# A twelve-layer decoder on one core: the choice of tokens counts in the compare, the experts' norm moves to the middle stage, and gathers, adds, stores, expert products and unread products are put in another order

## The reference

```
scores = softmax(x @ gate_w.T)                    # 4096 tokens x 8 experts
kept_w, kept_idx = top_k(scores.T, k=512)         # each expert takes its 512 best tokens
y = x[kept_idx]
y = (y - mean(y)) * rsqrt(var(y) + 1e-5) * ln_w + ln_b
h = gelu(y @ fc1[e].T + b1[e])                    # 128 -> 512
out = (h @ fc2[e].T + b2[e]) * kept_w             # 512 -> 128
x = x.at[kept_idx].add(out)
```

## Time and profile before

| | us |
|---|---|
| median of 3 runs | 3353.27 |
| lowest, highest | 3339.86, 3361.25 |
| the profiled execution's own time | 3361.68 |
| its span, first to last instruction | 3359.5 |
| mean granted TensorE clock | 0.901 |
| PE busy | 2578.9 (77%) |
| PEld busy | 1833.1 (55%) |
| DVE busy | 1724.8 (51%) |
| ACT busy | 994.8 (30%) |
| POOL busy | 345.1 (10%) |

### The profile page before, as it was taken

The page is one execution under the profiler, slowest core; times in us unless marked ns, Lnnn a source line. Parts: engine busy times, 40 slices in busy tenths (PEclk is TensorE's granted clock), DMA queues, the critical chain, the costliest instruction groups (busy, mean ns, idle before and its releaser), DMA issues.

```text
span 3359.5 us, 52344 instructions
## 1 busy us (share of the span) xinstructions
PE 2578.9 (77%) x22728; PEld 1833.1 (55%) x22736; DVE 1724.8 (51%) x4110; ACT 994.8 (30%) x1385; POOL 345.1 (10%) x581
## 2 busy tenths in 40 slices
PE   4666468888888886366677779887798777987778
PEld 3444147777777775244555554655555555565554
DVE  5655735565665654631357541675416754167541
ACT  3333312222322221021132432324323243232432
POOL 0111100000000000065111000110001100011000
PEclk8788559999999998577898999989999899998999
DMA  2000000000000001112610000000000000000000
GB/s 81 1 1 1 2 1 1 8 8 8 1 8 8 8 8 48 45 30 44 160 40 1 1 7 0 1 1 1 7 0 1 1 1 7 0 1 1 1 1 25
DMA packets 39351, 48.09 MB, mean 14 GB/s; under 512 B 7169, under 2 KB 36369, under 8 KB 38354
## 3 DMA queue, kind: packets, MB, share of 16 engines
q1 hardware_dynamic: 33490, 40.43, 4.1%
q0 software_dynamic: 5632, 4.33, 1.0%
HBM read 31.81 MB, written 12.91 MB: 13 GB/s over the span
## 4 chain that ended last, share of the span: by engine, by line
PE 57%; DVE 30%; ACT 6%; issue 4%; POOL 2%; DMA 1%; SPq 0%; DVEq 0%; POOLq 0%; ACTq 0%
PE banks L2390 7%; PE banks L887 6%; DVE wide_area L2266 4%; PE banks L2589 3%; DVE wide_area L1744 2%; PE banks L2379 2%; PE banks L1387 2%; PE banks L2164 2%; PE banks L1352 2%; PE banks L1186 2%; DVE xs L916 2%; DVE weights L2083 1%; PE banks L1420 1%; PE banks L584 1%; PE banks L1671 1%
## 5 line engine op out<-in xcount | busy, mean ns | idle before, releaser
L2589 PE MATMUL banks<-wA 128*128 128x128 f32 x2362 | 317.7, 288 | 4.2 <-ACT xf L948 2.1
L2589 PEld LDWEIGHTS banks<-wA 128*128 128x128 f32 x2362 | 296.8, 202 | 23.4 <-issue 16.3
L908 DVE BATCH_NORM_STATS2 stats<-banks 128x6 f32<-128x128 f32 x208 | 46.3, 285 | 397.3 <-PE banks L887 362.9
L2266 DVE TENSOR_REDUCE wide_area<-banks 128x8 f32<-128x2048 f32 x64 | 146.7, 2293 | 106.7 <-PE banks L2164 106.7
L923 POOL TENSOR_TENSOR rstd<-moments,eps 128x4 f32<-128x4 f32 x56 | 11.1, 199 | 1438.4 <-DVE moments L912 1438.4
L2247 ACT ACTIVATE weights<-banks 128x2048 f32<-128x2048 f32 x64 | 120.1, 1877 | 99.2 <-PE banks L2173 99.2
L1744 DVE TENSOR_REDUCE wide_area<-banks 128x16 f32<-128x1024 f32 x80 | 94.1, 1218 | 53.2 <-PE banks L1657 53.1
L2390 PE MATMUL banks<-wide_area,big 128*128 128x512 f32 x192 | 85.7, 592 | 0.0
L916 DVE TENSOR_SCALAR xs<-banks,moments,rstd 128x128 f32<-128x128 f32 x208 | 70.8, 403 | 27.0 <-POOL rstd L925 25.5
L2083 DVE TENSOR_TENSOR weights<-banks,wC 128x2048 f32<-128x2048 f32 x32 | 72.2, 2286 | 23.9 <-PE banks L1970 23.9
L908 DVE BATCH_NORM_STATS2 dilvals<-banks 128x6 f32<-128x128 f32 x144 | 32.0, 284 | 94.6 <-PE banks L887 94.6
(11 more groups left out here) (756 smaller groups left out, 6140.3 us busy)
## 6 DMA issues: line engine op xcount, KB each, us to landing
big<-in_wE SPq DMA_DIRECT2D x1, 4096.0 KB, 12.5
weights<-long_kernel SPq DMA_DIRECT2D x8, 512.0 KB, 7.2
conv<-wide_area SPq DMA_DIRECT2D x16, 256.0 KB, 2.7
wC<-in_wC SPq DMA_DIRECT2D x1, 3012.0 KB, 15.4
wC<-in_wG SPq DMA_DIRECT2D x1, 2971.0 KB, 19.2
big<-in_wT SPq DMA_DIRECT2D x1, 2560.0 KB, 11.5
x_all<-in_xT SPq DMA_DIRECT2D x1, 2048.0 KB, 8.5
rows<-spread SPq DMA_DIRECT2D x8, 256.0 KB, 2.5
```

The source lines that it names most:

```text
L908: dve.bn_stats(m.stats[:, i, :], self.tokens(i)).then_inc(*sg.up("dve", f"stats{i}"))
L2266: return dve.tensor_reduce(m.peaks[:, k % 2, :, :].rearrange("p t (r c) -> p r t c", r=4)[:, :, :, SPARE[j]], m.bank[:, :, :].rearrange("p ...
L2589: pe.matmul(bank[:, 0:P], m.ident, m.ident, start=True, stop=True)
```

## The change

- **Choice.** `try` and `count` go. The compare writes its sum as a second output (`accum_out`). Both possible next trials, `higher` and `lower` (int32 operations on 128x1), are computed while TensorE adds the counts; `keep` multiplies the flag with `higher`, and `try` takes the maximum with `lower`.
- **Unread products** at six new places: 8 before the choice's first product, 4 before its rounds, 3 behind each of its 30 sums, 24 behind the rank's last product and ahead of the chunks, 20 before `features(0)`, 5 before `hidden(0)`.
- **Norm.** The experts' norm leaves the expert stage. A new `LaneRows` on GpSimd computes, for each group in the middle stage, the factor by which the far lane's normed tokens have to be multiplied to be normed once more (four operations on 128x4, one of them a power) and multiplies 128x512 tokens by it. It stands between `LaneNorm` and `LaneGate` on GpSimd. `store_rows` stores `total` first, then waits for this product and stores it to `rows`. The lead lane's norm on VectorE waits for `LaneRows` of two groups before, since they share small tiles.
- **Experts.** The gathered rows go to TensorE straight from the buffers, of which there are six. GpSimd issues 16 gathers ahead of the first `add`, and behind `add(0)` to `add(4)` 4, 4, 3, 3 and 2. TensorE's order is features(0), hidden(0), features(1), out(0), hidden(1), features(2), hidden(2), and then, for `e` from 1, features(e+2), out(e), hidden(e+2). VectorE has only `weighted` left and reads the gate value from the buffer.
- **Mask work** (L3310 to L3321) moves behind `experts.dve`.

```diff
@@ Choice.dve, the rounds
-            dve.tensor_tensor(m.own_trial.bitcast(I32), m.own_level.bitcast(I32), self.bits.bitcast(I32)[:, it:it + 1],
-                              ALU.bitwise_or).then_inc(*bt.up("dve", "try"))
-            dve.wait_ge(*bt.done("dve", "try", it))
-            dve.tensor_scalar(m.own_flags, m.own_probs, m.own_trial, None, ALU.is_ge).then_inc(*bt.up("dve", "atleast"))
-            dve.wait_ge(*bt.done("dve", "atleast", it))
-            dve.tensor_reduce(m.own_count, m.own_flags, AX, ALU.add).then_inc(*bt.up("dve", "count"))
+            dve.tensor_scalar(m.own_flags, m.own_probs, m.own_trial, 0.0, ALU.is_ge, ALU.add, accum_out=m.own_count)\
+               .then_inc(*bt.up("dve", "atleast"))
+            dve.tensor_tensor(high, trial, bits[:, it + 1:it + 2] if more else trial, ALU.bitwise_or).then_inc(*bt.up("dve", "higher"))
+            dve.tensor_tensor(low, trial, m.own_pairs.bitcast(I32)[:, it:it + 1] if more else bits[:, it:it + 1], ALU.bitwise_xor)\
+               .then_inc(*bt.up("dve", "lower"))
+            dve.wait_ge(*bt.done("dve", "lower", it))
             dve.wait_ge(*bt.done("pe", "sum", it))
-            dve.scalar_tensor_tensor(out=m.own_trial, in0=m.Z[:, 0:1], scalar=float(CAPACITY), in1=m.own_trial,
+            dve.scalar_tensor_tensor(out=m.own_kept, in0=m.Z[:, 0:1], scalar=float(CAPACITY), in1=m.own_high,
                                      op0=ALU.is_ge, op1=ALU.mult).then_inc(*bt.up("dve", "keep"))
             dve.wait_ge(*bt.done("dve", "keep", it))
-            dve.tensor_tensor(m.own_level, m.own_level, m.own_trial, ALU.max).then_inc(*bt.up("dve", "level"))
-            dve.wait_ge(*bt.done("dve", "level", it))
+            dve.tensor_tensor(m.own_trial, m.own_kept, m.own_low, ALU.max).then_inc(*bt.up("dve", "try"))
+            dve.wait_ge(*bt.done("dve", "try", it))
@@ Choice.pe
+        m.keep_busy(pe, m.S[1][:, 0, :], "choice start")
...
+        m.keep_busy(pe, m.S[1][:, 0, :], "choice same")
         for it in range(BITS):
-            pe.wait_ge(*bt.done("dve", "count", it))
+            pe.wait_ge(*bt.done("dve", "atleast", it))
             pe.matmul(m.Z[:, 0:1], m.same, m.own_count, start=True, stop=True).then_inc(*bt.up("pe", "sum"))
+            m.keep_busy(pe, m.S[1][:, 0, :], "choice bit")
...
+        m.keep_busy(pe, m.S[1][:, 0, :], "choice rank")
@@ Experts
-    BUFFERS = 3
+    BUFFERS = 6
+    AHEAD, BETWEEN = 16, (4, 4, 3, 3, 2, 0, 0, 0)
@@ Experts.pool
-        gather(0)
-        gather(1)
-        root(0)
-        gather(2)
-        root(1)
+        for k in range(self.AHEAD):
+            gather(k)
+        at = self.AHEAD
         for e in range(EXPERTS):
-            if e + 3 < EXPERTS:
-                gather(e + 3)
-            if e + 2 < EXPERTS:
-                root(e + 2)
             add(e)
+            for k in range(at, at + self.BETWEEN[e]):
+                gather(k)
+            at += self.BETWEEN[e]
@@ Experts.pe
         def features(e):
-            pe.wait_ge(*tk.done("dve", f"scaled{NT - 1}", e))
+            pe.wait_ge(*self.landed(e))
...
-        for e in range(2):
-            features(e)
-            hidden(e)
-        for e in range(EXPERTS):
+        m.keep_busy(pe, m.S[0][:, 0, :], "taken")
+        features(0)
+        m.keep_busy(pe, m.S[0][:, 0, :], "chosen")
+        hidden(0)
+        features(1)
+        out(0)
+        hidden(1)
+        features(2)
+        hidden(2)
+        for e in range(1, EXPERTS):
+            if e + 2 < EXPERTS:
+                features(e + 2)
             out(e)
             if e + 2 < EXPERTS:
-                features(e + 2)
                 hidden(e + 2)
@@ Experts.dve: moments, scaled and the copy of the gate value go; weighted reads self.taken(e)[:, i, D + e:D + e + 1]
@@ BUSY
+ 'taken': 20, 'chosen': 5, 'choice start': 8, 'choice same': 4, 'choice bit': 3, 'choice rank': 24
@@ new
+class LaneRows:
+    def pool(self, pool, n, scaled, written):
+        m, sg = self.lane, self.sig
+        pool.wait_ge(*scaled)
+        pool.tensor_tensor(self.factor, m.moments[:, :, 1], m.rstd, ALU.mult).then_inc(*sg.up("pool", "part"))
+        pool.wait_ge(*sg.done("pool", "part", n))
+        pool.tensor_tensor(self.factor, self.factor, m.rstd, ALU.mult).then_inc(*sg.up("pool", "var"))
+        pool.wait_ge(*sg.done("pool", "var", n))
+        pool.tensor_tensor(self.factor, self.factor, m.eps4[:, :], ALU.add).then_inc(*sg.up("pool", "eps"))
+        pool.wait_ge(*sg.done("pool", "eps", n))
+        pool.tensor_tensor(self.factor, self.factor, m.minus_half[:, :], ALU.pow).then_inc(*sg.up("pool", "root"))
+        pool.wait_ge(*sg.done("pool", "root", n))
+        pool.wait_ge(*written)
+        pool.tensor_tensor(self.rows, m.xs, self.factor.unsqueeze(2).broadcast_to([P, NT, D]), ALU.mult).then_inc(*sg.up("pool", "rows"))
@@ lead_dve
+            if later(it, 2):
+                dve.wait_ge(*far_rows.sig.done("pool", "var", it - 2))
@@ far_pool
             yield from far_norm.pool(pool, it)
+            far_rows.pool(pool, it, far_norm.sig.done("dve", f"scaled{NT - 1}", it), (saved, it * 48 + 16))
@@ store_rows
-                for dst, row in ((rows_dram, Experts.ROW), (total_dram, D)):
-                    sp.dma_start(bass.AP(dst.tensor, it * T * row, [[row, P], [P * row, NT], [1, D]]), far.xs[:, :, :])\
-                      .then_inc(saved, 16)
+                sp.dma_start(bass.AP(total_dram.tensor, it * T * D, [[D, P], [P * D, NT], [1, D]]), far.xs[:, :, :]).then_inc(saved, 16)
+                sp.wait_ge(*far_rows.sig.done("pool", "rows", it))
+                sp.dma_start(bass.AP(rows_dram.tensor, it * T * Experts.ROW, [[Experts.ROW, P], [P * Experts.ROW, NT], [1, D]]),
+                             rows_normed).then_inc(saved, 16)
@@ the vector engine's list
             choice.dve(dve)
+            experts.dve(dve)
             dve.memset(m.ones3, 1.0).then_inc(*ready_g.up("dve", "ones3"))
...
-            experts.dve(dve)
```

More of the change, by code:

```diff
@@ L339, in __init__ @@
         self.iota, self.token, self.block = iota, token, block
-        self.setup = Signals(ctx, nc, "choice_setup", dve="ones tri ones_f expert0 expert1 level turned_block same probs all_levels",
+        self.setup = Signals(ctx, nc, "choice_setup", dve="ones tri ones_f expert0 expert1 pairs first turned_block same probs all_levels",
                              pe="turned_block probs same level")
-        self.bit = Signals(ctx, nc, "choice_bit", dve="try atleast count keep level", pe="sum")
+        self.bit = Signals(ctx, nc, "choice_bit", dve="atleast higher lower keep try", pe="sum")
         scans = " ".join(f"scan{e}" for e in range(EXPERTS))
@@ L518, in __init__ @@
         self.rows, self.total = rows, total
-        self.take = Signals(ctx, nc, "take", dve=tile_steps("stats", "aggr", "scaled") + " weight", pool="eps rstd", pe="features",
-                            act="out")
+        self.take = Signals(ctx, nc, "take", pe="features", act="out")
         self.hid = Signals(ctx, nc, "hidden", pe="h0 h1 h2 h3", act="g0 g1 g2 g3")
@@ L527, in hidden, with taken, landed, gather @@
         return self.mem.wide_q[:, FC * (e % 2) + c, :]
+    def taken(self, e):
+        return self.mem.taken[e % self.BUFFERS]
+    def landed(self, e):
+        return self.gathered[e % self.BUFFERS], 16 * NT * (e // self.BUFFERS + 1)
     def pool(self, pool, slots_ready, rows_ready):
[L530 to L544 removed]
+        m, rs = self.mem, self.res
+        def gather(k):
+            e, i = divmod(k, NT)
+            if e >= self.BUFFERS and i == 0:
+                pool.wait_ge(*rs.done("dve", f"weighted{NT - 1}", e - self.BUFFERS))
+            pool.indirect_dma_start(self.taken(e)[:, i, :], None, self.rows,
+                                    bass.IndirectOffsetOnAxis(ap=m.slots[:, k:k + 1], axis=0))\
+                .then_inc(self.gathered[e % self.BUFFERS], 16)
         def add(e):
@@ L624, in gelu @@
                                bias=self.b1[:, e * FC + c:e * FC + c + 1]).then_inc(*hd.up("act", f"g{c}"))
-        for e in range(EXPERTS):
+        affine(0)
+        gelu(0)
+        for e in range(1, EXPERTS):
             affine(e)
@@ L830 @@
 MIDDLE = "nfnfnfnfnfnfnfnfnfnffnfnfnnfnnfnnnffffnfnffnffnn"
-BUSY = {'first1': 2, 'dil_sum0': 7, 'wide scores1': 8, 'lead norm': 10, 'near norm': 1, 'dil_peaks1': 12, 'dil_peaks0': 2, 'lead product': 5, 'wide start': 2, 'gate': 7, 'back0': 3, 'first3': 1, 'first0': 1, 'first norm': 6, 'last norm 0': 9, 'last norm 1': 12, 'last norm 2': 9, 'last norm 3': 12, 'last norm 4': 12, 'last norm 5': 8, 'last norm 7': 1, 'last norm 8': 8, 'retention turned': 7, 'quant whole': 2}
```

(7 more changed lines are left out.)

69 lines of the change are left out of this document (17 added, 52 removed).

## The result

| | before | after |
|---|---|---|
| median of the runs (16 and 16) | 3358.9 us | 3334.4 us |
| lowest and highest | 3339.9, 3362.2 | 3324.0, 3344.5 |
| profiled execution, span | 3359.5 | 3334.4 |
| ratio, 95% interval | | 0.9931 (0.9918 to 0.9944) |

The change gains 24.5 us, 0.7%: within 1% by the bound named in the prediction, and inside its range (3296 to 3338), but 14.5 us short of the 39 that it forecast. From the forecast's 3314 to 3334.4 it is 20.4 us; the remaining 6 are the base: the three runs known then had a median of 3353.3, sixteen have 3358.9.

The account below looks back on a forecast made before the run. Choice bound by a chain of short steps, experts by TensorE with a hole in each; 20 + 2 + 18.8 - 2 = 39 us off 3361.7 gives 3322.7, or 3314 from the median 3353.3; 8-in-10 range 3296 to 3338.

Parts of the forecast that it names:

- the bound named in the prediction: Whole kernel: about 1% is what a measurement can tell from no change; within 1% was given 0.32.
- The round: Choice: a round falls from 2.07 to 1.39 us, saving 20 us over 30 rounds.
- first rival: Choice: TensorE's clock stays low despite unread products, nothing saved in the rounds, time 3339; chance 0.12.
- The rest of the choice: Choice outside its rounds: the high clock shortens the first chunk's and four more product waits, saving 2 us.
- The experts: Expert stage, from the slots to the read-back: 147.8 us falls to 129, saving 18.8.
- The walk: Experts: following GpSimd's and TensorE's queues in order, with stalls of 13 and 9 us at features(6) and features(7), giving 129.
- the old hole: Experts before the change: 3.8 us of TensorE waiting for weighted and scaled, after which hidden(3) took 6.51 against 3.70.
- GpSimd's queue slower than its rows: Rival, experts: an add's period is 2.1 instead of 1.84, experts end at 135, time 3320; chance 0.13.
- No stalls: Rival, experts: quicker gathers, no stalls at features(6) and features(7), experts take 111, time 3298; chance 0.08.
- The mask work: Moved beside add(6) and add(7), VectorE's mask work slows GpSimd's adds; 2 us charged.
- The middle stage: GpSimd's 3.3 us of new row work in each of eight groups costs nothing, covered by 12.3 us idle.
- The forecast's own range: Whole kernel: 3304 to 3326, from the compare's bounds and two or three us on the experts' stalls.

Follow-up runs that it names:

- experiment 2: Changed kernel without the unread products at the choice's start and in its rounds, those of the rank kept; 3339.7 us against the changed kernel's 3334.4.
- Experiment 5: Changed kernel with 8, 24 and 30 unread products in TensorE's waits before features(5), (6), (7); ratio 0.9904 to the kernel before, 3329 us.
- experiment 3: Changed kernel with gathers earlier, four behind each of the first four adds; ratio 0.9850 to the kernel before, 3311 us.
- experiment 4: Changed kernel with TensorE's old order, out(e) ahead of features(e + 2), gathers as in the change; ratio 0.9849 to the kernel before, 3309 us.
- experiment 10: Changed kernel with both experiment 3's gathers and experiment 4's TensorE order, 20 unread products before features(0); ratio 0.9835 to the kernel before, 3308 us.
- experiment 7: Experiment 6's kernel with 32 unread products instead of 20 ahead of features(0); ratio 0.9875 to the kernel before.
- experiment 8: Experiment 7's kernel with eight more unread products ahead of features(6); ratio 0.9880 to the kernel before.
- experiment 6: Changed kernel with 17 gathers ahead of the adds, then 5, 4, 4 and 2 behind the first four; ratio 0.9852 to the kernel before.
- experiment 9: Experiment 10's kernel with 32 unread products instead of 20 ahead of features(0); ratio 0.9887 to the kernel before.
- Experiment 12: Changed kernel with VectorE's mask work back between choice and experts, beside the first gathers; ratio 0.9928 to the kernel before.
- experiment 11: Changed kernel with GpSimd's rows product made seven times over in each middle-stage group; one execution, span 3367.1 us, 32.7 more than the changed kernel.

## Why the prediction was right and wrong

**The round (forecast 1.39, measured 1.42): right.** The count reached TensorE after 0.54 us, as charged; the record of the compare is 0.48, followed by one of 0.08 named as a read of the accumulator, which begins before the first one's record ends. This is the rule of the Trainium skill, VectorE: DVE Perf Modes, section on two Vector instructions with no wait between them: an operation that writes its accumulator is two instructions. The trace agrees, with 0.08 for the second. From the compare's start to `keep` it was 1.03 us, where the forecast has 0.54 + 0.47 = 1.01. `higher` and `lower` cost nothing: behind them VectorE still waits 0.40. The saving was 0.65 in 26 rounds and 0.35 on average in the first four, in which the clock was still low: 18.3 of the 20.

**The clock (first rival, 0.12): right for the rounds.** Unread products raised it to 1.00, and experiment 2 without them stands at 0.50. The clock is worth 5.9 us of the choice (81.7 against 87.6). What the forecast left out is that the clock came up late, with four rounds of 1.72 on average.

**The rest of the choice (2 us): right in sum**; 20.1 in all against 22.

**The experts (forecast 18.8, measured 6.0): the mechanism right, one term mis-sized.** The walk had the stalls before `features(6)` and `(7)` and their circle, and the waits are there (features(6) 7.2 us, features(7) 8.4; forecast 13 and 9, with features(5) waiting till 49.1, measured 51.1). The step that was off is the last one: "the product set behind a hole ran slower by 2.8 us in the rows [...]; two us for each stall gives 129". It took the size from `hidden(3)`, which followed the old hole. In the new order, `features` and the whole `out` follow the wait: 40 records in four tiles, and an out goes from 6.1 to 11.0 us. That is 4.9 and not 2, with half a us more for `features`, and it falls three times, since the 2.1 us before `features(5)` cost the clock too. The first time it costs the 3.6 us that GpSimd waits before `add(3)`. The other two cost 5.5 and 5.4: from the gather's landing to the end of `out(4)` and of `out(5)` it is 12.1 us, in the walk 6.5 and 6.7. Together 14.5 instead of 4, which is 10.5 of the 12.8 us by which 141.8 misses 129. Some 2 more were there before `add(3)`: GpSimd was free for it 60.8 us behind the slots and not 58.9. They begin at `out(0)` (20.7 us behind the slots, not 18.7, with `features(0)` and the unread products behind the first wait at the low clock). Experiment 5 took the first and the last of the three away, 3.6 + 5.4, and gained 8.9.

**GpSimd's queue slower than its rows (0.13): no.** A gather took 0.95 and an add 1.56 to 1.65, with 0.30 between.

**No stalls (0.08), 3298:** not so in the change, but it is what experiments 3, 4 and 10 came near to, at 113 to 121 us for the experts (the rival had 111). With 111 the forecast's own terms give 3296 or 3297 and not 3298.

**The mask work (2 us): too high for this kernel, and in part by luck.** Beside it, `add(6)` and `add(7)` took 1.56 to 1.65; the median of all is 1.56. But in other kernels an add beside it took 1.94 to 2.53. Which it is goes, in all ten kernels with the mask work in this place, with who starts first; no experiment moved the start by itself. Here, the add starts 0.11 us ahead of the mask's first instruction (`whole_h`, at 1547.38); in experiment 3 it starts 0.13 us behind it (1518.01):

```profile
1547.27 1.65 POOL L559 DMA_INDIRECT total<-heads,smalls  x1 [0.30 <-issue]
```

```profile
1518.14 2.53 POOL L559 DMA_INDIRECT total<-heads,smalls  x1 [0.30 <-issue]
```

In experiments 2, 4, 7 and 8 the add starts 0.1 ahead and takes 1.64 or 1.65; in 5, 6, 9 and 10 it starts 0.1 to 0.3 behind and takes 1.96, 2.52, 1.94 and 2.39. Experiment 12 shows the price on gathers, 1.9 us over sixteen, with the first of them 0.3 us behind the mask's first instruction. The Trainium skill, SBUF — State Buffer, section "SBUF: two separate sides", says that GpSimd can't write descriptors while VectorE holds the shared ports in some of its modes; the gathers agree, and so do the adds that start behind the mask's first instruction. The forecast's 2 us were the price of the whole stretch of the mask on gathers; on adds it was 0.2 us here and about 1 in experiments 3 and 10.

**The middle stage (0): right, on a wrong measure.** Idle time of 12.3 us was taken as cover, though 7.4 of it comes before the work's own input (experiment 11).

**The range: held, in part by luck.** The forecast's own range, 3304 to 3326, is missed: two or three us for the experts' stalls were too few, and the base moved 5.6 us up. The wider one, 3296 to 3338, holds 3334 because it was stretched to the rival in which the choice's clock stays low, and that did not happen.

## What to carry to other kernels

An idle stretch of TensorE has two prices: its length, and what the next product set loses at the low clock. The second is sized by what stands behind the wait in the new order, here 4.9 us for a set of small products of 6.1 us, and 2.0 for `hidden(6)` in experiment 4, and not by what stood behind an old one. Where two in-order queues feed each other, follow the circle: put the work that the other engine needs ahead of the wait for that engine, on either side, and most of the stall goes. And count the cover of added work from the moment its own input is there to the moment its engine is needed, not by the whole idle time in the view.

## What the runs showed of the hardware

- Short waits of TensorE for a gather were followed by the low clock (0.50) in most places: 2.09 and 2.70 us in the changed kernel, 2.21 in experiment 3, 2.54 in 4, 2.65 in 6, 2.48 in 7, 2.38 in 8. One of 2.49 in experiment 7 was not (1.00 behind it, `out(4)` 6.1 us), nor were those of 0.95, 1.30 and 1.42 in experiments 8, 3 and 5. What the low clock cost depended on what came next: 4.9 us where it was an out, 2.0 where it was `hidden(6)`, and behind the first wait of the changed kernel it was over before `out(0)`, which took 6.1:

```profile
1425.67 1.12 PE L581 MATMUL banks<-wA,keys 128*128 128x128 f32 x4 [2.70 <-DMA keys<-rows,smalls]
```

- An indirect add that starts just behind VectorE's first mask instruction takes 1.94 to 2.53 us (five kernels), one that starts 0.1 us ahead of it 1.64 or 1.65 (five kernels), one with nothing of VectorE beside it 1.55 to 1.57.
- Twelve more unread products (2.9 us by their records) in a wait of 2.6 us delayed the first out by 11 and 14 us in the two pairs of kernels that differ in them alone, and all three kernels with them, run on one chip, had the delay. Filling a wait to the brim can cost more than the wait; the cause is open.
- A compare of 128x256 with a sum as second output costs 0.48 and 0.08 us, where the compare alone was 0.35 and the reduce 0.42.
